# Small tiles of the second heads transposed by DMA in a fused attention and feed-forward kernel, with the key-value parts, first output weights, signs and magnitudes moved

## The reference, cut to what matters

```python
q_lat = x @ Wq_down                                   # 512 -> 256
q = concat(q_lat @ Wq_up, rope(q_lat @ Wq_rope))      # 16 heads of 64 + 64
kv_lat = x @ Wkv_down                                 # 512 -> 128
k = concat(kv_lat @ Wk_up, rope(x @ Wk_rope))
v = kv_lat @ Wv_up                                    # 16 heads of 128
attn = softmax(causal(q @ k.T * HD ** -0.5))
x = x + (attn @ v) @ Wo                               # x normalised before attention
wq = clip(round(w / mean(abs(w))), -1, 1) * mean(abs(w))   # W_up, W_gate, W_down
x = x + (silu(h @ wu.T) * (h @ wg.T)) @ wd.T          # h = layernorm(x)
```

## Time and profile before

| | before |
|---|---|
| median of 3 runs | 1763.58 us (1761.55 to 1764.98) |
| profiled execution, its own time | 1764.33 us |
| span of the profile | 1762.5 us |
| PE busy | 1697.7 us, 96% |
| DVE / ACT / POOL busy | 1205.6 / 1049.9 / 834.9 us (68 / 60 / 47%) |
| latents and projections | to about 302 us |
| attention | about 302 to 1400 us |
| feed-forward | about 1400 us to the end |
| mean granted clock of PE | 0.988 of full speed |

### The profile page before, as it was taken

The page is one execution under the profiler, slowest core; times in us unless marked ns, Lnnn a source line. Parts: engine busy times, 40 slices in busy tenths (PEclk is TensorE's granted clock), DMA queues, the critical chain, the costliest instruction groups (busy, mean ns, idle before and its releaser), DMA issues.

```text
span 1762.5 us, 30735 instructions
## 1 busy us (share of the span) xinstructions
PE 1697.7 (96%) x9762; PEld 1367.1 (78%) x9762; DVE 1205.6 (68%) x2815; ACT 1049.9 (60%) x2543; POOL 834.9 (47%) x635
## 2 busy tenths in 40 slices
PE   6899997899999999999999999999999999999998
PEld 5788775677777777777877877877887778888887
DVE  6466775588778787788888888888888733334332
ACT  3233334688788787778787787778777522323222
POOL 2466565344345368677677677577565300000000
PEclk9999998899999999999999999999999999999999
DMA  3399987887677665667657657557555630000000
GB/s 128 114 229 220 237 221 203 184 199 146 144 154 143 125 130 131 145 132 148 125 129 148 128 120 157 123 123 151 121 107 126 192 143 1 25 1 25 0 25 24
DMA packets 390010, 225.94 MB, mean 128 GB/s; under 512 B 305888, under 2 KB 339808, under 8 KB 389600
## 3 DMA queue, kind: packets, MB, share of 16 engines
q1 hardware_dynamic: 378336, 203.05, 50.4%
q10 hardware_dynamic: 11520, 20.98, 4.3%
HBM read 97.06 MB, written 54.53 MB: 86 GB/s over the span
## 4 chain that ended last, share of the span: by engine, by line
PE 61%; POOL 9%; ACT 4%; issue 3%; DVE 3%; DMA 2%; SPq 0%; ACTq 0%; POOLq 0%; DVEq 0%
PE ps_scores L1650 15%; PE ps_o L1710 14%; PE ps_scores L1872 13%; PE ps_scores L1728 7%; PE ps_scores L1691 5%; PE ps_scores L1887 3%; PE ps_o L1887 3%; POOL halved L1217 3%; ACT probs L1457 2%; POOL below L1414 2%; POOL signs L1418 1%; POOL k_lo L1359 1%; POOL signs L1422 1%; DMA signs<-in_W_up 1%; ACT halved L1468 1%
## 5 line engine op out<-in xcount | busy, mean ns | idle before, releaser
L1457 ACT ACTIVATE probs<-ps_scores,bias 128x512 f32<-128x512 f32 (+3 forms) x640 | 397.9, 628 | 106.5 <-DVE bias L1561 85.7
L1217 POOL TENSOR_TENSOR halved<-probs,halved 128x512 f16<-128x512 f32 (+3 forms) x320 | 320.9, 1017 | 251.8 <-ACT halved L1468 240.5
L1710 PE MATMUL ps_o<-moved,kv_hi 128*128 128x256 f16 x2176 | 335.0, 275 | 0.6 <-DMA moved<-halved 0.6
L1551 DVE TENSOR_REDUCE negmax<-ps_scores 128x1 f32<-128x512 f32 (+1 forms) x384 | 251.5, 673 | 52.6 <-PE ps_scores L1650 52.4
L1710 PEld LDWEIGHTS ps_o<-moved,kv_hi 128*128 128x128 f16 x2176 | 184.2, 98 | 96.8 <-issue 73.9
L1650 PE MATMUL ps_scores<-k_hi,q_hi 128*128 128x512 f32 (+2 forms) x576 | 244.2, 424 | 7.7 <-ACT probs L1457 7.0
L1473 ACT CAST moved<-ps_scores 128x512 f16<-128x512 f32 (+3 forms) x320 | 167.6, 524 | 102.9 <-PE ps_scores L1691 100.4
L1599 DVE TENSOR_TENSOR moved<-ps_scores,moved 128x512 f16<-128x512 f32 (+3 forms) x320 | 193.4, 604 | 48.2 <-ACT moved L1473 46.9
L1650 PE MATMUL ps_scores<-k_hi,q_lo 128*128 128x512 f32 (+2 forms) x576 | 214.1, 372 | 0.0
L1710 PE MATMUL ps_o<-moved,kv_lo 128*128 128x256 f16 x1088 | 213.2, 273 | 0.0
L1650 PE MATMUL ps_scores<-k_lo,q_hi 128*128 128x512 f32 (+2 forms) x576 | 213.1, 370 | 0.0
(11 more groups left out here) (165 smaller groups left out, 3513.7 us busy)
## 6 DMA issues: line engine op xcount, KB each, us to landing
plainT<-plain_out ACTq DMA_DIRECT2D x64, 256.0 KB, 4.5
rotT<-rot_out SPq DMA_DIRECT2D x64, 256.0 KB, 4.4
all_signs<-signs SPq DMA_DIRECT2D x24, 512.0 KB, 3.2
q_raw<-plainT SPq DMA_DIRECT2D x128, 64.0 KB, 2.4
q_raw<-rotT SPq DMA_DIRECT2D x256, 32.0 KB, 2.1
signs<-in_W_up SPq DMA_DIRECT2D x16, 512.0 KB, 4.2
signs<-in_W_gate SPq DMA_DIRECT2D x16, 512.0 KB, 3.9
signs<-in_W_down SPq DMA_DIRECT2D x16, 512.0 KB, 4.0
```

The lines of the kernel that those rows point to most:

```text
L1217: nc.gpsimd.tensor_tensor(halved_of(args, pair, 1), by_block(probs_of((n, i, 0, p), pair)), halved_of(args, pair, 0), ALU.subtract).then_i ...
L1457: nc.scalar.activation(probs_of(args, pair), ps_scores[:, pieces.number[args] % RING, 0:keys], ACT.Exp, scale=-1.0 if last_piece(*args) el ...
L1551: nc.vector.tensor_reduce(to, scores, AX_X, ALU.max, negate=True).then_inc(max_done, 1)
L1710: last = nc.tensor.matmul(ps_o[:, i, 0:2 * P], kv[x][:, b, :], there, start=(s == 0 and (m, b) == (0, blocks[0])), stop=(s + 1 == nsteps(t ...
```

## The change

Small tiles (i = 1) of head 1 leave PE: `by_dma` is true for head 0 and for every small tile, and these pieces take the way by `halve_high`, `halve_low` and a move of their own. Events of this way now have the arguments (n, i, h, p), and a unit `moved` is filled by two moves, or by a move and a turn; `units` counts the units, and `moved_in` has one semaphore per `halved` buffer. The table `TIMES` has new numbers throughout. The key-value parts are made two chunks in the fifth and two in the sixth pair's projections, and none in the seventh. `load_w_first` and `stores_over` are due earlier and its split later. The magnitudes of odd chunks go to DVE. The signs of pair 2 are spread further, and each load of a sign chunk is due closer to its first instruction.

```diff
-def kv_order(first, both=False):
-
-    after = {(PLAIN, 0, 0): [(KV, "high", first)], (PLAIN, 0, 1): [(KV, "low", first)], (PLAIN, 3, 1): [(KV, "turn", first)]}
-    if both:
-        after[PLAIN, 1, 1] = [(KV, "high", first + 1)]
-        after[PLAIN, 2, 0] = [(KV, "low", first + 1)]
-        after[PLAIN, 3, 1].append((KV, "turn", first + 1))
+def kv_order(first):
+
+    after = {(PLAIN, 0, 0): [(KV, "high", first)], (PLAIN, 0, 1): [(KV, "low", first)],
+             (PLAIN, 1, 1): [(KV, "turn", first), (KV, "high", first + 1)], (PLAIN, 2, 0): [(KV, "low", first + 1)],
+             (PLAIN, 3, 0): [(KV, "turn", first + 1)]}
     return [e for entry in usual_order() for e in (entry, *after.get(entry, ()))]
...
-    ORDERS = (usual_order(), last_order(), kv_order(0), kv_order(1), kv_order(2, both=True))
+    ORDERS = (usual_order(), last_order(), kv_order(0), kv_order(2))
     USUAL, LAST = range(2)
-    BEHIND = (2, 3, 4, LAST)
+    BEHIND = (2, 3, USUAL, LAST)
...
+def by_dma(n, i, h, p):
+
+    return h == 0 or i == 1
+
...
-            "halved_hi": (-7.18, -6.86, -5.87, -5.11, -0.98),
-            "turn": (-3.27, -1.92, -0.52, 1.87, 3.95),
+            "halved_hi": (-7.47, -6.72, -5.97, -5.03, -0.89, -0.53),
+            "turn": (-2.96, -1.56, -0.24, 1.16),
...
-                for p in range(npieces(t)):
-                    for kind in ("halved_hi", "halved_lo", "move", "turn", "turned_hi", "turned_lo"):
-                        put(kind, i, p)
+                        for kind in (("halved_hi", "halved_lo", "move") if by_dma(n, i, h, p) else
+                                     ("turn", "turned_hi", "turned_lo")):
+                            put(kind, i, h, p)
...
-        self.only[0] += [(0.2, 0, "split_w", (0,)), (1.9, 0, "stores_over", ()), (3.5, 0, "load_w_first", (1,)),
-                         (5.0, 0, "split_w", (1,))]
+        self.only[0] += [(0.2, 0, "split_w", (0,)), (0.5, 0, "stores_over", ()), (1.5, 0, "load_w_first", (1,)),
+                         (5.6, 0, "split_w", (1,))]
         self.only[0] += [(4 + 12 * m, 0, "load_y", (m + 1,)) for m in range(NC - 1)]
         self.only[ABS_PAIRS] += [(16.2, 0, "sum_abs", ()), (16.3, 0, "scale", ())]
         for n in range(CHUNKS):
             pair, k = divmod(n, SIGNS_A_PAIR)
-            at = 24 + 11.5 * k if pair == 0 else 6 + 17 * k
+            at = 20 + 15 * k if pair == 0 else 6 + 17 * k
             events = self.only[ABS_PAIRS + pair]
-            events.append((at - 5, 0, "load_sign", (n,)))
+            events.append((at - 3.2, 0, "load_sign", (n,)))
             events += [(at + 2 * part, 0, "sign", (n, part)) for part in range(3)]
-            events.append((at + 5.8, 0, "store_sign", (n,)))
+            events.append((at + 6.2, 0, "store_sign", (n,)))
...
+    units = plan.count("move", lambda n, i, h, p: h == 0)
...
-    moved_in = [sem(f"moved_in{j}") for j in range(MOVED)]
+    moved_in = [sem(f"moved_in{j}") for j in range(HALVED)]
...
+    def unit_of(n, i, p, pair):
+
+        return units.total((n, i, 0, p), pair) - 1
+
     def moved_of(args, pair):
-        return moved[(moves.total(args, pair) - 1) % MOVED][:, 0:nblocks(*args)]
+
+        n, i, h, p = args
+        return moved[unit_of(n, i, p, pair) % MOVED][:, 0:nblocks(*args), :, h * P:(h + 1) * P]
...
     def until_probs_free(engine, args, pair):
 
-        n, i, h, p = args
-        if h == 0:
-            engine.wait_ge(halved_lo_ready, lows.total((n, i, p), pair))
+        if by_dma(*args):
+            engine.wait_ge(halved_lo_ready, lows.total(args, pair))
         else:
-            engine.wait_ge(turn_ready, turns.total((n, i, p), pair))
+            engine.wait_ge(turn_ready, turns.total(args, pair))
 
     def halve_low(pool, args, pair):
-        n, i, p = args
         pool.wait_ge(halved_hi_ready, highs.total(args, pair))
-        nc.gpsimd.tensor_tensor(halved_of(args, pair, 1), by_block(probs_of((n, i, 0, p), pair)), halved_of(args, pair, 0),
+        nc.gpsimd.tensor_tensor(halved_of(args, pair, 1), by_block(probs_of(args, pair)), halved_of(args, pair, 0),
                                 ALU.subtract).then_inc(halved_lo_ready, 1)
...
-                if kind == "abs":
+                if kind == "abs" and args[0] % 2 == 0:
...
+                if kind == "abs" and args[0] % 2:
+                    n, = args
+                    dve.wait_ge(abs_loaded, 16 * (n + 1))
+                    nc.vector.tensor_reduce(abs_sums[:, n // PAIRS, n % PAIRS:n % PAIRS + 1], signs[:], AX_X, ALU.add,
+                                            apply_absolute_value=True).then_inc(abs_done, 1)
...
                     for p in sorted({piece_of(t, b) for b in blocks}):
-                        pe.wait_ge(turned_lo_ready, turns.total((n, i, p), pair + f))
-                        until_moved(pe, (n, i, p), pair + f)
+                        for h in range(2):
+                            if by_dma(n, i, h, p):
+                                until_moved(pe, (n, i, h, p), pair + f)
+                            else:
+                                pe.wait_ge(turned_lo_ready, turns.total((n, i, h, p), pair + f))
```

More of the change, by code:

```diff
@@ L944 @@
[L944 to L958 removed]
+            "scores": (-10.89, -10.18, -9.79, -9.01, -7.45, -6.68, -5.9, -4.93, -2.72, -2.14),
@@ L1708, in body @@
                             p = piece_of(t, b)
-                            there = moved[(moves.total((n, i, p), pair + f) - 1) % MOVED][:, b - cuts(t)[p], z, :]
+                            there = moved[unit_of(n, i, p, pair + f) % MOVED][:, b - cuts(t)[p], z, :]
                             last = nc.tensor.matmul(ps_o[:, i, 0:2 * P], kv[x][:, b, :], there,
```

261 lines of the change are left out of this document (129 added, 132 removed).

## The result

The change made the kernel slower: 1795.24 us in the median of 4 runs (1792.26 to 1798.16), against 1762.57 (1761.37 to 1764.98) in the same comparison. The ratio is 1.0184, 95% interval 1.0163 to 1.0204, or 32 us (29 to 36). The forecast was 1724, the range 1707 to 1748.

A forecast was written before the change was run, and what follows sets the result against it. The prediction took PE's work as the bound within attention. Its terms, -31.7 + 4 - 6 - 3 - 2.5 - 1 = -40.2 us, took 1764.3 us to 1724 us, range 1707 to 1748.

The forecast's parts named there:

- Turns taken off PE: On PE, 288 small-tile turns removed at 0.11 us each, all on the path: -31.7 us, upper bound 46.3.
- What takes them up: On POOL, 12 more halvings a pair, 11 us, mostly hidden: +4 us, nothing at best, 9 at worst.
- The moves: On SP and the DMA engines, 12 more moves a pair, 12 us of DMA time: no price.
- Signs: Signs of pair 2 set further apart: -1 us, bounds +2 and -2.
- First output weights and key-value parts: PE's waits in pair 0 and at the seventh pair's end shrink through earlier loads: -6 and -3 us.
- Magnitudes: In the first two stretches, twelve of ACT's 24 magnitudes go to DVE: -2.5 us, bounds 0 and -5.
- (c): Slower: SP's in-order queue makes moves and query loads late, a pair takes 139 us: 1796 us, chance 0.06.
- (b): POOL gives part back: exponentials wait for buffers at every fourth added halving, 24 us in place of 4: 1744, chance 0.18.
- (a): Turns taken off PE free more, 0.161 us each, 14.6 us more in all: 1709 us, chance 0.15.
- (d): No change: PE's freed time turns into waits because ACT's exponentials set the pace: 1764 us, chance 0.03.

The follow-up runs named there:

- the edges alone: The kernel before with the first output weights and key-value parts (`kv_order`) of the change and nothing else: 1752.56 us, -10.4 us.

## Why the prediction was wrong

- **Turns taken off PE** (-31.7) is the first step that failed. Its count and its 0.11 us were right (four turns are 0.44 us on the chain after, too: `876.49 0.44 PE ps_scores L1702 x4`). Wrong was "all of it on the path while PE is the bound": 192 turns taken away, with nothing put in their place, gave 0.054 us each, so 288, scaled, are -15.6. PE idle for 0.9% says that PE is full now. It doesn't say how soon the next limit comes when it has less to do: at 1.1 us a pair others were there. Which they are was not tested.
- **What takes them up** (+4). The halvings measured +9.9 (6.4 to 13.3, scaled), near the upper bound of 9.
- **The moves** (no price) measured +17.1 (13.7 to 20.3, scaled). "The small tile's products come late in the slot" holds for its own products. What was overlooked is the cost for others: every move holds SP's queue 1.25 us and the DMA engines, and the large tiles' moves behind it land later. With these three terms the exchange is -15.6 + 9.9 + 17.1 = +11.4, a loss by itself, if costs measured in the kernel before and in its order may be added. Per turned block, 0.054 us on PE are exchanged for (9.9 + 17.1) / 288 = 0.094 us by POOL and DMA. The rule that I set aside, in the Trainium skill's "VectorE: DVE Perf Modes", sections "The three transpose paths" and "Rules for kernel authors" (TensorE if PSUM will do, DMA otherwise), came out right, though neither of its durations is what decided here.
- **Signs** (-1, bounds 2) is the step with the largest error. The edit from 5 to 3.2 stood in the diff and I costed the spacing alone. With early loads the account is -9.2 for the other parts and +11.4 for the exchange, thus +2, measured -2.1, within the intervals. The late loads then add 34.5 us, and that makes the +32.4 of the result. The price needs both: the load at 3.2 steps, which was worth -1.4 and +2.5 us where no moves were added, and the added moves ahead of it.
- **First output weights and key-value parts** (-9) held: -10.4. PE's waits of 4.70 and 3.78 us are gone as forecast, but not for nothing: the stop for ACT behind the second is 7.4 us where it was 4.4, and PE still waits 3.8 us once for probabilities. How the 10.4 divide between the two was not tried.
- **Magnitudes** (-2.5, bound 0) measured nothing: with the turns moved -2.1 with half of them on DVE and -3.3 with none, and without the turns, together with the spacing, 1.2 us more than the edges alone. One costs DVE 1211 ns, under the 1.4 us forecast.

The rivals: (c) named the place, SP's queue in order, and its 139 us a pair were near the 140.0 measured. Its reason fell all the same. It took the waits that remain at moves as the measure, 0.65 us each. Measured are 0.68 in the change (283.3 / 416), but 0.64 (265.2 / 416) in the run with early loads, where a pair is 134.9 us. The formula would give 138 there. SP has the time; what counts is what stands ahead of a load that another in-order engine needs, and whether that thing waits for the same engine. (b) had the sign of POOL's part, with 24 us where my term had 4: with early loads ACT waits for POOL 18.1 us, 27 times, where it was 14.5 us, 15 times, and taking 188 us off POOL gave 5 to 8. (a) is out: a turn taken away frees less than 0.11 us and not more. (d) had the time of the run with early loads, and that PE's freed time turns into waits is in part what the run with fewer turns shows; its reason, the pace of ACT's exponentials, was not tested.

Three things stay open. From 780 us on, the late loads cost 28 us in the change and 19 in the kernel before with added moves, for about the same waits of POOL. The two differ by the added halvings, the turns and the order; POOL is at 75% of the last stretch in the change ("417.96" of 560), before it was at 69%; and the granted clock is 0.98 in the one and 1.00 in the other, which over 560 us would be about 11 us, an estimate from these two figures. It was not tried with halvings and moves both added. Nor was the new order priced by itself, and the spacing and the store times of the signs, which make the 14 us together, were not tried apart; SP's wait for the store speaks for the spacing.

## What to carry to other kernels

When work is added to an in-order queue, look for every load in it whose user waits in order too, and for what the instructions ahead of that load wait for: if it is the same engine, a due time that was harmless closes a loop, and here one number was worth 34 us. Take the price of removed work from a run in which it is removed and nothing is put in its place; here an engine that was 99% busy gave back about half of what it was freed of. And cost each number of a diff, above all those that look like tuning.

## What the runs showed that I had not expected

- Transposes that nobody reads cost 15.0 us for 84, or 0.18 us each, with the DMA share only at 0.72; one-block transposes of the same count 7.9 us. A DMA transpose holds SP's queue about 1.25 us at either size (medians 1288 and 1241 ns).
- 36 turns fewer a pair on an engine that is 99% busy left the pair at 134.9 us in the run with early loads. That is a mean of two things: from 780 us on there are 1719 products where there were 1703, a pair of 132.9 us and no longer 134.2, and from 500 to 640 us only 397 where there were 426.
- The granted clock does not follow PE's idle share alone. In the change it was 0.98 from 500 to 640 us (8.3 of 140 us idle) and from 780 to 1340 us (4.3% idle), but 1.00 from 640 to 780 us (8.0 of 140 us idle). With early loads, idle 6.3 of 560 us, the last stretch is at 1.00 again, as before. In the kernel before with the late loads and the added moves PE was idle 25.4 of 560 us, more than the 24.0 of the change, and it was at 1.00 too. So part of what the waits cost in the change may have been taken a second time by the clock, by my estimate about 2% of the stretches that show 0.98, and a sum of waits doesn't hold it.
